# Graph attention: addresses of the first gathers from sorted keys in SBUF, chunks prepared three ahead, and a rearranged end

## What is computed

```python
messages = x[col]                                  # col = dst, row = src
gate = messages @ W_gate.T + b_gate
h = messages @ W_lin.T + b_lin
seg_max = segment_max(gate[:, 0], row)
e = exp(gate[:, 0] - seg_max[row])
attn = e / (segment_sum(e, row) + 1e-16)[row]
pooled = segment_sum(attn[:, None] * h, row)
out = layernorm(x + pooled @ W_out.T + b_out)
```

## Time and profile before

| | us |
|---|---|
| median of three runs | 2586.03 |
| the profiled execution | 2590.55 |
| its span | 2588.7 |
| DVE busy | 1715.4 (66%) |
| POOL busy | 1669.4 (64%) |
| PE busy | 1219.9 (47%) |
| ACT busy | 656.1 (25%) |
| mean granted TensorE clock | 0.617 |

### The profile page before, as it was taken

One profiled execution on the slowest core, in us unless ns is written; L12 is line 12 of the kernel. 1 busy time (PEld: TensorE's weight loads), 2 busy tenths in 40 slices (PEclk: granted clock), 3 DMA queues, 4 the chain that ended last, 5 costly groups with the idle time before them and its releaser, 6 DMA issues.

```text
span 2588.7 us, 29156 instructions
## 1 busy us (share of the span) xinstructions
PE 1219.9 (47%) x5733; PEld 1064.7 (41%) x5733; DVE 1715.4 (66%) x6933; ACT 656.1 (25%) x2151; POOL 1669.4 (64%) x1715
## 2 busy tenths in 40 slices
PE   5711455555555454565545434444543444454620
PEld 4511344544444444454434434434443443344610
DVE  9998776777678776576745645654554565455687
ACT  3300222322322232104223213212321321231115
POOL 1004777777777777763777777777777777776034
PEclk8655555556556556676666666665666666566665
DMA  3022222222222222231222222222222222222232
GB/s 129 1 101 51 52 54 54 54 53 54 54 54 54 53 63 55 55 127 44 56 55 55 56 54 55 55 55 55 55 55 54 55 55 55 54 54 80 73 93 78
DMA packets 92093, 156.61 MB, mean 60 GB/s; under 512 B 29177, under 2 KB 61285, under 8 KB 91415
## 3 DMA queue, kind: packets, MB, share of 16 engines
q0 software_dynamic: 53152, 110.66, 19.1%
q1 hardware_dynamic: 38040, 43.90, 5.0%
q10 hardware_dynamic: 732, 0.20, 0.0%
HBM read 134.36 MB, written 20.28 MB: 60 GB/s over the span
## 4 chain that ended last, share of the span: by engine, by line
POOL 55%; issue 21%; DVE 17%; PE 5%; DVEq 1%; DMA 0%; ACT 0%; ACTq 0%; POOLq 0%
POOL ring L564 55%; DVE nodes_sb L1139 5%; DVE first_keys L1030 3%; DVE first_keys L1031 3%; PE bank L852 2%; DVE spread L1134 1%; DVE shift L1256 1%; PE bank L833 1%; PE bank L822 1%; DVE ring L1238 1%; DVE stats L1244 1%; DMA ring<-node_table,gather_at 0%; PE bank L795 0%; DVE late_keys L1031 0%; DVE late_keys L1030 0%
## 5 line engine op out<-in xcount | busy, mean ns | idle before, releaser
L564 POOL DMA_INDIRECT ring<-node_table,gather_at x1661 | 1596.8, 961 | 561.4 <-issue 505.0
L852 PE MATMUL bank<-ring,spread 128*128 x3712 | 771.8, 381 | 406.6 <-DVE nodes_sb L1139 327.9
L852 PEld LDWEIGHTS bank<-ring,spread 128*128 128x128 f32 x3712 | 690.4, 282 | 481.7 <-issue 480.9
L1134 DVE TENSOR_SCALAR spread<-iota_row,places 128x128 f32<-128x128 f32 x1856 | 553.6, 299 | 369.9 <-PE bank L852 346.9
L1139 DVE SCALAR_TENSOR_TENSOR nodes_sb<-nodes_sb,drops,bank 128x130 f32 x1856 | 647.1, 349 | 5.4 <-issue 3.6
L651 ACT ACTIVATE ring<-ring,weights 128x129 f32<-128x129 f32 x1664 | 497.4, 394 | 3.3
L669 ACT ACTIVATE weights<-bank 128x40 f32<-128x40 f32 x42 | 8.6, 204 | 1026.5 <-PE bank L816 1026.5
L1104 DVE TENSOR_TENSOR_SCAN run_max<-pen,bank 40x128 f32<-40x128 f32 x42 | 17.3, 412 | 354.7 <-PE bank L802 354.7
L795 PE MATMUL bank<-ended,ones 40*128 40x40 f32 x376 | 87.5, 404 | 197.5 <-DVE ended L984 197.5
L795 PEld LDWEIGHTS bank<-ended,ones 40*128 40x128 f32 x376 | 81.9, 318 | 206.8 <-issue 206.8
L802 PE MATMUL bank<-ident,ring 128*40 128x128 f32 x42 | 16.1, 384 | 252.9 <-DMA ring<-node_table,gather_at 252.9
(11 more groups left out here) (162 smaller groups left out, 1070.5 us busy)
## 6 DMA issues: line engine op xcount, KB each, us to landing
ring<-node_table,gather_at POOLq DMA_INDIRECT x1661
ring<-kept_sums SPq DMA_DIRECT2D x14, 455.0 KB, 5.4
node_table<-ring SPq DMA_DIRECT2D x1, 6347.7 KB
nodes_sb<-in_x SPq DMA_DIRECT2D x10, 625.0 KB
kept_sums<-nodes_sb SPq DMA_DIRECT2D x2, 2600.0 KB, 8.3
ring<-in_x SPq DMA_DIRECT2D x10, 448.0 KB, 6.0
out<-ring SPq DMA_DIRECT2D x10, 448.0 KB
k<-sorted_keys SPq DMA_DIRECT2D x126, 20.0 KB
```

Source lines behind the costliest of these rows:

```text
L564: pool.indirect_dma_start(out=chunk_rows[c % RING][:, t, :], out_offset=None, in_=table[:, :], in_offset=bass.IndirectOffsetOnAxis(ap=gath ...
L852: last = pe.matmul(tile_ps(slot), lhsT=spread[:, slot, :], rhs=ring[:, bass.ds(got[slot], ROW)], start=True, stop=True)
L1134: return dve.tensor_scalar(spread[:, slot, :], iota_row[:, :], places[r % 2][:, t:t + 1], None, ALU.is_equal)
```

## The change

- `sort_orders` puts no steps of set 1 between those of set 0. All 42 short ones go to the front of `late`, and `SORT_AHEAD` is 104.
- Set-up that isn't needed for the first keys (`set_windows`, `set_places`, `set_blocks`) moves from ahead of `build_keys` to three places in the sort, each ahead of a step that waits for a turned group.
- `read_first_dst`: chunk 0's addresses are taken from the sorted keys of group 0 in SBUF, and PE and ACT turn and copy them ahead of the last turn of the sort. `prepare(0)` and `find_ended(0)` move ahead of its last four steps.
- The blanking of `sums` goes from one POOL copy to seven ACT copies behind turns.
- One key buffer `k3` in place of two; what `prepare` makes is kept for three chunks (`PREPS`), rows for five (`ROW_SETS`). Chunk 18 is prepared in round 16, and every later one three chunks ahead. SP loads chunk 1's keys behind the store of group 1.
- In rounds without a chunk, PE does `sum_ended` behind batch 1 and `choose_rows` behind batch 3, and DVE does `place_slots` at its batch 3.
- The end is cut in two (`FINAL`: blocks 0 to 55, 56 to 97). The first part's maxima are compared at the start of round 46 and its shares made behind batch 3. POOL scales both the old sums (in place) and the new ones; PE adds x and the old sums into PSUM through the identity; DVE adds that to POOL's product (`join`).

```diff
-SORT_AHEAD = 64
-FILL = 2
+SORT_AHEAD = 104
+PREPS = 3
+ROW_SETS = 5
+BLANKS = 7
+FINAL = ((0, 56), (56, BLOCKS))
 def prepared_in(r):
-    if r + 2 < FIRST_CHUNK[1] + 2:
+    if r + 2 < FIRST_CHUNK[1] + PREPS:
         return r + 2
     h, n = set_of_round(r)
-    c = FIRST_CHUNK[h] + n + 2
+    c = FIRST_CHUNK[h] + n + PREPS
...
-    for steps in stretches(0):
-        ahead += steps + short[:FILL]
-        short = short[FILL:]
+    ahead += [step for steps in stretches(0) for step in steps]
...
             def load_chunk(c):
-                if c >= 2:
-                    sp.wait_ge(k3_used, c - 1)
+                if c >= 1:
+                    sp.wait_ge(k3_used, c)
...
             load_chunk(0)
-            load_chunk(1)
             store_keys(0, 1)
             sp.wait_ge(part_stored[0][1], 16)
             for g in range(3):
                 load_x(g, tail_in[0])
-            for c in range(2, FIRST_CHUNK[1]):
+            for c in range(1, FIRST_CHUNK[1]):
                 load_chunk(c)
...
-            pool.tensor_copy(sums.rearrange("p (b w) -> p b w", w=ROW),
-                             blank_row[:, :].unsqueeze(1).to_broadcast([P, BLOCKS, ROW])).then_inc(sums_blank, 1)
-            pool.wait_ge(sums_blank, 1)
+            pool.wait_ge(sums_blank, BLANKS)
             for c in range(CHUNKS):
-                pool.wait_ge(prep_copied, c + 1)
+                pool.wait_ge(*((prep_copied, c + 1) if c > 0 else (first_dst_copied, 1)))
...
             for g in range(GROUPS):
+                blocks = slice(g * GB, (g + 1) * GB)
+                pool.wait_ge(dens_ready, 1 if blocks.stop <= FINAL[0][1] else 2)
+                pool.wait_ge(tail_in[kept_load[g]], 16 * loads_in[kept_load[g]])
+                pool.tensor_tensor(kept_at[g][:, :, 1:WIDTH], kept_at[g][:, :, 1:WIDTH],
+                                   kept_scale[:, blocks].unsqueeze(2).to_broadcast([P, GB, FEAT]), ALU.mult).then_inc(kept_scaled, 1)
                 if g >= Z:
                     pool.wait_ge(out_ready, g - Z + 1)
...
-                pool.wait_ge(x_mixed, g + 1)
-                pool.tensor_tensor(mixed[g % Z], mixed[g % Z], x_at[g], ALU.add).then_inc(resid_ready, 1)
...
             for n, step in enumerate(turnings(first_order)):
+                if n == len(turnings(first_order)) - 1:
+                    pe.wait_ge(first_dst_ready, 1)
+                    pe.nop(nofuse=True)
+                    pe.transpose(prep_ps, dst_f[:, :], ident[0:T, 0:T]).then_inc(first_dst_turned, 1)
                 turn(*step)
...
+                    if chunk_of(r) is None and r + 1 < ROUNDS:
+                        if b == 1:
+                            sum_ended(r + 1)
+                        if b == 3:
+                            choose_rows(r + 1)
                     if b == PLACES_AT and prepared_in(r) is not None:
                         turn_prep(prepared_in(r), r + 1)
...
+            for g in range(GROUPS):
+                pe.wait_ge(tail_in[x_load[g]], 16 * loads_in[x_load[g]])
+                pe.wait_ge(kept_scaled, g + 1)
+                if g >= 2:
+                    pe.wait_ge(resid_ready, g - 1)
+                pe.nop(nofuse=True)
+                for ps, blocks in tail_banks(g):
+                    pe.matmul(ps, lhsT=ident[:, :], rhs=x_at[g][:, blocks, :], start=True, stop=False)
+                    last = pe.matmul(ps, lhsT=ident[:, :], rhs=kept_at[g][:, blocks, 1:WIDTH], start=False, stop=True)
+                last.then_inc(x_mixed, 1)
...
+            def read_first_dst():
+                after_last(0, 0)
+                dve.tensor_scalar(dst_r[:, :], rows[0][1][0:T, 0:P].bitcast(I32), DST_MASK, None, ALU.bitwise_and)
+                dve.drain()
+                dve.tensor_copy(dst_f[:, :], dst_r[:, :])
+                dve.drain().then_inc(first_dst_ready, 1)
...
+            waits_for_turn = {(0, 0, LOG_COLS + 1, "turned", 0): set_windows, (0, 1, LOG_COLS + 1, "turned", 0): set_places,
+                              (0, 0, LOG_COLS + 2, "turned", 0): set_blocks}
...
                 if n == 8:
                     build_keys(1)
+                if n == len(first_order) - 4:
+                    prepare(0, 0)
+                    find_ended(0)
+                if done[0][0] == all_steps and done[0][1] < all_steps and not first_read:
+                    read_first_dst()
+                    first_read = True
+                if step in waits_for_turn:
+                    waits_for_turn[step]()
                 sort_step(*step)
-            prepare(0, 0)
-            find_ended(0)
             place_slots(0)
             prepare(1, 1)
...
+                if r == ROUNDS - 1:
+                    dve.wait_ge(sums_added, slots_upto(r) + 2 * BATCH)
+                    compare_maxes(0)
                 for b in range(2, max(end, PLACES_AT + 1)):
                     if b < end:
                         spread_batch(r, b, at, (r, b - 2))
+                    if b == 3 and chunk_of(r) is None and r + 1 < ROUNDS:
+                        place_slots(r + 1)
...
+                    if r == ROUNDS - 1 and b == 3:
+                        join_shares(0)
...
+            compare_maxes(1)
+            join(0)
+            measure(0)
+            join_shares(1)
+            for g in range(1, GROUPS):
+                join(g)
+                scale_and_shift(g - 1)
                 measure(g)
             scale_and_shift(GROUPS - 1)
```

More of the change, by code:

```diff
@@ new lines, in join_shares @@
+            def join_shares(n):
+                cols = slice(*FINAL[n])
+                dve.wait_ge(shares_ready, n + 1)
+                dve.tensor_tensor(kept_den[:, cols], kept_den[:, cols], kept_scale[:, cols], ALU.mult)
+                dve.tensor_tensor(none[:, cols], sums_of[:, cols, 0], fresh_scale[:, cols], ALU.mult)
+                dve.drain()
+                dve.tensor_tensor(kept_den[:, cols], kept_den[:, cols], none[:, cols], ALU.add)
+                dve.drain()
+                dve.reciprocal(inv_den[:, cols], kept_den[:, cols])
+                dve.drain()
+                dve.tensor_tensor(fresh_scale[:, cols], fresh_scale[:, cols], inv_den[:, cols], ALU.mult)
+                dve.tensor_tensor(kept_scale[:, cols], kept_scale[:, cols], inv_den[:, cols], ALU.mult)
+                dve.drain().then_inc(dens_ready, 1)
@@ L1242, in measure, with join @@
+            def join(g):
+                dve.wait_ge(pooled_ready, g + 1)
+                dve.wait_ge(x_mixed, g + 1)
+                for ps, blocks in tail_banks(g):
+                    here = mixed[g % Z][:, blocks, :]
+                    dve.tensor_tensor(here, here, ps, ALU.add)
+                dve.drain().then_inc(resid_ready, 1)
             def measure(g):
```

272 lines of the change are left out of this document (140 added, 132 removed).

## The result

The changed kernel takes **2494.77 us** (median of 4 executions, 2492.18 to 2503.55) against 2586.45 us of the kernel before beside it: a ratio of 0.9655, 95% interval 0.9629 to 0.9682. The profiled execution took 2495.45 us with a span of 2493.6, so 95 us went out of the span. I had predicted 2486, with a range of 2462 to 2522.

A forecast was written before the change was run, and what follows sets the result against it. POOL's gathers, one per 1.25 us, were taken as the bound, their pace untouched. Gains of 29 + 39 + 1 + 31 = 100 us cut the span from 2588.7 to 2489, median about 2486; forecast 2470 to 2500, wider 2462 to 2522.

The forecast's parts named there:

- Start: From kernel start to chunk 2's gathers: first gather 46 us earlier, chunk 2 at 308 against 337.45, gain 29 us (20 to 35).
- the wait for chunk 1's keys: In the start: with a single key buffer, DVE waits for the second chunk's keys, +9 us (5 to 10).
- Why I don't count 46: In the start: chunk 2's addresses need round 0 on DVE, so of 46 us at the first gather 29 us count.
- Between the sets: At the boundary of the two sets: the 46.9 us wait before chunk 18 goes; gain 39 us (29 to 45).
- X: Time at which chunk 15's gathers end, 1051.7 in the kernel before; boundary times are counted from it.
- s: What the three rounds without a chunk (16 to 18) save, taken as 10 us (0 to 16).
- The wait for the ring: Before chunk 21: a new wait until chunk 16's row slot is free, 16 - s, about 7 us.
- Behind the last gather: From the last gather to the last sum: round 45 saves 4 us, round 46 adds 3; net +1 (-4 to +5).
- POOL's scaling runs there beside DVE's sums: In round 46: POOL scales while DVE sums, with no cost counted for the overlap.
- Tail: From the final sums to the end: 4.6 us a group instead of 6.49, 76 us for 107, 31 us less.
- the rival that it bounds the tail: In the tail: PE's clock stays low or swings, 6 to 7.7 us a group, 2503 to 2523 us; chance 0.17.
- The rival in which a busy VectorE stretches every gather: Gathers behind chunk 1 take 1.32 us each, costing 120 us; the kernel ends slower, at 2606; chance 0.04.

The follow-up runs named there:

- e_fillers: Changed kernel with 42 short sort steps back between the first set's turnings and 64 late steps ahead of round 0; 3892.21 us, 0.9980 of the kernel before.
- e_two_ahead: Changed kernel preparing chunks two ahead of their round instead of three, on chip A; 3814.47 us, 0.9909 of the kernel before.
- f_two_ahead: Same kernel as e_two_ahead, on chip B; 3825.45 us, 0.9911 of the kernel before.
- experiment 3: Changed kernel with ScalarE scaling the first three groups in round 46, GpSimd starting after the last shares, chunk 1's keys loaded early; 3863.64 us, 0.9919 of the kernel before.
- experiment 4: Changed kernel with the tail's mixing of x put back on VectorE, GpSimd adding, early shares kept; 3874.69 us, 1.0041 of the kernel before.
- f_pool_late: Changed kernel with GpSimd's first tail scaling held until all but the last eight sums of round 46 are added, chip B; 3847.54 us, 0.9974 of the kernel before.
- before_again: The kernel before, unchanged, run and profiled on chip B; 3853.94 us, 1.0004.
- again: The changed kernel, unchanged, run on chip C; 3900.2 us, 1.0007 of the kernel before there.

## Why the prediction came out, and its one step that failed

Measured in the two profiled executions, against the terms of the sum:

- **Start, 29 us predicted, 24.3 measured** at chunk 2. The first gather came at 188.7 for a predicted 185. Round 0's softmax came at 286.57 for 281, chunk 2 at 313.2 for 308, behind 17.7 us of waiting for its addresses where I had said some 15; the wait for chunk 1's keys was 10.0 for 9. So 3.7 of the 5.6 us by which round 0 was late stood already at the first gather, in the sort of group 0. "Why I don't count 46" was right: 42.8 us at the first gather became 24.3 at the third chunk. At the end of set 0's gathers the gain was 27.9 (1051.7 to 1023.8), the rest having come in between.
- **Between the sets, 39 predicted, 36.4 measured** (chunk 22 starts 64.3 us earlier, less 27.9). With X now at 1023.8, round 19's softmax at 1140.7 is X + 117; before it was X + 123.8, and preparing chunk 18 in round 16 was to add 3.3, so s is 10, as taken. The wait for the ring was 11.2 for a predicted 6: 2.4 of the 5.2 us are that round 22 began at X + 240.4 and not at X + 238 (a round took 41 us, not 40.3), 1.6 that POOL was ready sooner, at X + 250.4. No run undid the start or this part at the pace of the profiles, so these two gains, two thirds of the whole, rest on the two traces, not on an experiment. Where the early first gather and the third chunk ahead were undone on the slower chips (e_fillers, e_two_ahead, f_two_ahead), no time was lost.
- **Behind the last gather, +1 predicted with -4 to +5, -6.7 measured.** This is the step that failed. From the end of the last gather to the last sum it took 107.0 us for 100.3. Round 45 gave 6.2 us for a predicted 4, the rounds ahead of it 0.9. The sentence "POOL's scaling runs there beside DVE's sums" treated the two as free of each other, a term put at nothing without a reason. Round 46 grew by 13.8 us: the compare and the shares are some 3 of it, as predicted, and the spreads 10.2 (experiment 3). I had the rule in hand: I cited the Trainium skill, page SBUF — State Buffer, for operations with two SBUF inputs, and checked only those. The section "Who interferes with whom" on that page of the Trainium skill also names `tensor_scalar` as one that can take the pair of ports shared with GpSimd, and the spread is a `tensor_scalar`. The rows agree: 0.28 us becomes 1.46 beside a multiplication of 1.68.
- **Tail, 31 predicted, 34.9 measured.** A group takes 4.3 us (14 joins, 2428.1 to 2480.1 for twelve of the distances) for 4.6; VectorE's terms were near (additions 1.2, statistics 2.0, shift and reciprocal 0.44), and so were POOL's. That the exchange of engines makes the tail shorter is shown (experiment 4). PE stayed at the faster level, so the rival that it bounds the tail didn't occur. Below are one group's matmuls in the tail's middle (timeline of PE) and the windows view of ten us around them. Its value behind the five engines is the granted clock: 1.00, the level of 2.4 GHz.

```profile
2451.52 1.10 PE L924 MATMUL bank<-ring,ident 128*128 128x512 f32 x2 [0.96 <-POOL ring L578]
2452.45 1.02 PE L925 MATMUL bank<-ring,ident 128*128 128x512 f32 x2
2453.31 0.81 PE L924 MATMUL bank<-ring,ident 128*128 128x384 f32 x2
2453.95 0.81 PE L925 MATMUL bank<-ring,ident 128*128 128x384 f32 x2
```

```profile
2450.00:2460.00 10.00, 7.05 (x18) 2.86 (x16) 8.42 (x40) 7.26 (x20) 7.92 (x5) 1.00 0.37 109
```

A group's matmuls end 3.2 us behind their start (2451.5 to 2454.8) where I had reckoned 4.3, and ahead of them PE waits for POOL.

The rival in which a busy VectorE stretches every gather didn't occur either: a gather takes 958 ns on average, before 961.

The terms, with 2.6 us that the gathers behind chunk 22 gained (66.9 less 64.3), give the 95.1 (27.9 + 36.4 + 2.6 - 6.7 + 34.9), 4.9 us less than the 100 of the forecast: 7.7 of the failed step, 1.1 of the start and 2.6 of the boundary, less 3.9 of the tail and 2.6 of the gathers. That the error stayed so small is in part luck: the tail and the gathers happened to make good most of the failed step. The other 3.9 us between 2486 and 2494.8 are how far a profiled execution lies above its median: 4.5 us before, 0.7 after.

## What to carry to other kernels

When work is moved to GpSimd, list every VectorE instruction that will run beside it, not only those of the moved part. Here a short one could cost the whole length of the other engine's instruction, nine of them 10 us, and holding the burst back only moved it onto the next small operations. In a stretch in which VectorE is the bound, ScalarE did the same scaling without holding it. And a gain from earlier gathers must be expected only where gathers are what the rounds wait for: the same program gained 3.5% on one chip and nothing on chip C, while the part of it in which no gather runs gained 27 to 28 us on both.

## What the runs showed of the hardware that I had not expected

- A VectorE `tensor_scalar` of 128x128 fp32, one SBUF input and a scalar per partition, goes from 0.28 to as much as 1.46 us beside GpSimd's multiplications of 128x896, and ends with them; `tensor_scalar` and `tensor_tensor` of 42 columns go from 0.2 to 1.6 or 1.7 us (after and f_pool_late). Not lengthened beside them are additions with an input in PSUM (0.34 us in the sums, 0.69 in the joins), the statistics of 128 columns (0.28) and a reciprocal of 42 columns (0.42). ScalarE's 42 scalings (0.39 us each) lengthened no spread.
- Three chips ran the kernel before at 3853 to 3897 us, one at 2586. Instructions take the same time on both: a gather 951 to 972 ns on average in every profile, with its last packet 2.2 us behind its start. The difference is stalls of VectorE while gathers run, up to 27.4 us each in before_again; 1190.5 us of them stand ahead of the spreads in the profile of again. Their cause stays open.
